# Two up projections of a gated MLP, accumulated side by side instead of one after the other

## The reference

```
xn2 = rmsnorm(x, ln2_w)
s   = x + (silu(xn2 @ W1) * (xn2 @ W3)) @ W2      # W1, W3: 512 x 1408, W2: 1408 x 512
out = x0 + s * silu(ffn(xn))                      # the gate comes from an earlier stage
```

## Time and profile before

| | us |
|---|---|
| median of 3 runs | 1926.0 (1924.37 to 1926.05) |
| the profiled execution, its time | 1922.71 |
| its span | 1921.0 |
| TensorE busy | 1780.7 (93%) |
| VectorE busy | 922.4 (48%) |
| ScalarE busy | 545.1 (28%) |
| mean granted TensorE clock | 0.978 |

### The profile page before, as it was taken

How to read it: one execution, slowest core, us unless ns; L and a number is a source line. 1 busy time by engine, 2 the same in 40 slices (tenths; PEclk the granted TensorE clock), 3 DMA queues, 4 the chain that set the end, 5 groups by cost and what they waited for, 6 DMA issues and landing times. The chain is left out here.

```text
span 1921.0 us, 24333 instructions
## 1 busy us (share of the span) xinstructions
PE 1780.7 (93%) x9104; PEld 1319.7 (69%) x9104; DVE 922.4 (48%) x1336; ACT 545.1 (28%) x887; POOL 403.5 (21%) x353
## 2 busy tenths in 40 slices
PE   4999999778999999999998749999999999999998
PEld 3878888654656666565656438787878787777776
DVE  4464454255777768576777455514141413132322
ACT  3223333232424335242523133212121212121211
POOL 5780000025425251533425000000000000000000
PEclk9999999989999999999999779999999999999999
DMA  6342321110011010101011032220202020202020
GB/s 144 99 109 76 98 66 66 44 55 28 1 71 66 5 71 0 71 0 71 22 44 44 1 121 93 77 109 0 109 0 109 0 109 0 109 0 109 0 88 22
DMA packets 49040, 110.89 MB, mean 58 GB/s; under 512 B 12704, under 2 KB 24048, under 8 KB 40816
## 3 DMA queue, kind: packets, MB, share of 16 engines
q1 hardware_dynamic: 45104, 89.44, 13.9%
q10 hardware_dynamic: 2304, 16.78, 2.1%
q0 software_dynamic: 1600, 4.25, 1.1%
HBM read 76.89 MB, written 33.57 MB: 58 GB/s over the span
## 5 line engine op out<-in xcount | busy, mean ns | idle before, releaser
L1228 DVE TENSOR_TENSOR m_h<-m_ps,m_silu 128x512 f32<-128x512 f32 x88 | 60.8, 691 | 431.1 <-PE m_ps L1381 431.1
L1379 PE MATMUL m_ps<-m_xshi,m_w1hi 128*128 128x512 f32 x352 | 142.8, 406 | 7.6 <-DVE m_xslo L1221 6.0
L1353 POOL TENSOR_TENSOR m_sq_sum<-m_sq 128x512 f32<-128x512 f32 x8 | 10.8, 1352 | 658.5 <-ACT m_sq L1290 658.5
L1307 ACT ACTIVATE m_silu<-m_ps 128x512 f32<-128x512 f32 x88 | 52.4, 596 | 336.8 <-PE m_ps L1381 335.9
L1379 PE MATMUL m_ps<-m_xshi,m_w3hi 128*128 128x512 f32 x352 | 139.1, 395 | 2.4 <-ACT m_silu L1307 2.4
L1380 PE MATMUL m_ps<-m_xslo,m_w1hi 128*128 128x512 f32 x352 | 139.5, 396 | 0.0
L1381 PE MATMUL m_ps<-m_xshi,m_w1lo 128*128 128x512 f32 x352 | 139.5, 396 | 0.0
L1381 PE MATMUL m_ps<-m_xshi,m_w3lo 128*128 128x512 f32 x352 | 139.0, 395 | 0.0
L1380 PE MATMUL m_ps<-m_xslo,m_w3hi 128*128 128x512 f32 x352 | 139.0, 395 | 0.0
L978 PE MATMUL a_att<-a_qx,a_lv 128*32 128x512 f32 (+1 forms) x512 | 104.1, 516 | 22.4 <-DVE a_qxd L689 20.3
L818 POOL TENSOR_TENSOR a_qx<-a_lv,hmask 128x512 f32<-128x512 f32 x64 | 87.4, 1365 | 154.2 <-PE a_att L978 98.2
(11 more groups left out here) (242 smaller groups left out, 4195.1 us busy)
## 6 DMA issues: line engine op xcount, KB each, us to landing
row<-scratch_xn SPq DMA_DIRECT2D x16, 1024.0 KB, 4.8
row<-scratch_xmid SPq DMA_DIRECT2D x16, 1024.0 KB, 7.0
m_xt<-in_L_attn_W SPq DMA_DIRECT2D x33, 256.0 KB, 3.4
f_xt<-in_L_attn_x SPq DMA_DIRECT2D x8, 1024.0 KB, 7.5
scratch_xn<-row SPq DMA_DIRECT2D x8, 1024.0 KB, 6.3
scratch_gate<-row ACTq DMA_DIRECT2D x8, 1024.0 KB, 3.9
scratch_xmid<-row ACTq DMA_DIRECT2D x8, 1024.0 KB, 3.9
row<-scratch_gate SPq DMA_DIRECT2D x8, 1024.0 KB, 9.8
```

What stands on the lines that cost most here:

```text
L1228: dve.tensor_tensor(h[n], dense.region(f"b{j}"), silu[n], ALU.mult).then_inc(dense.taken_sem(f"b{j}"), 1)
L1307: act.activation(silu[n], dense.region(f"a{j}"), ACT.Silu).then_inc(dense.taken_sem(f"a{j}"), 1)
L1379: pe.matmul(ps, wh, xh, start=k == 0, stop=False)
```

## The change

In `up`, the loops over the two projections and over the four slices change places. Before, the 12 matmuls of a are issued, then the 12 of b. After, each slice gives 3 matmuls of a and 3 of b, in their two PSUM regions in turn. The waits for the weights of both and for the free regions of both now stand ahead of the first matmul of the block; the wait for a slice of the input stands ahead of the slice's first matmul, as before. Each projection still signals with its last matmul, which for a is now the fourth from the end of the block.

```diff
--- before.py
+++ after.py
@@ -1367,19 +1367,22 @@
                 pe.matmul(ps, avg_all, sq_sum, start=True, stop=True).then_inc(mean.ready_sem("ms"), 1)
 
             def up(i, j):
-                for n, (ab, w) in enumerate((("a", w1), ("b", w3))):
+                pair = (("a", w1), ("b", w3))
+                for n, (ab, w) in enumerate(pair):
                     pe.wait_ge(s_wlo, 3 * j + n + 1)
                     pe.wait_ge(*dense.free(f"{ab}{j}", i))
-                    ps = dense.region(f"{ab}{j}")
-                    for k in range(KT):
-                        if j == 0 and n == 0:
-                            pe.wait_ge(*count.at("xslo", i, k + 1))
+                for k in range(KT):
+                    if j == 0:
+                        pe.wait_ge(*count.at("xslo", i, k + 1))
+                    xh, xl = (a[:, k, :] for a in xs_hl)
+                    for ab, w in pair:
+                        ps = dense.region(f"{ab}{j}")
                         wh, wl = (a[:, k, j * P:(j + 1) * P] for a in w)
-                        xh, xl = (a[:, k, :] for a in xs_hl)
                         pe.matmul(ps, wh, xh, start=k == 0, stop=False)
                         pe.matmul(ps, wh, xl, start=False, stop=False)
                         ins = pe.matmul(ps, wl, xh, start=False, stop=k == KT - 1)
-                    ins.then_inc(dense.ready_sem(f"{ab}{j}"), 1)
+                        if k == KT - 1:
+                            ins.then_inc(dense.ready_sem(f"{ab}{j}"), 1)
 
             def down(i, j):
                 pe.wait_ge(*count.at("hlo", i, j + 1))
```

## The result

The changed kernel takes 1944.8 us (median of 4 runs, 1942.5 to 1946.0), the kernel before 1926.0 (median of 4, 1924.4 to 1928.2): a ratio of 1.0095 with a 95% interval of 1.0078 to 1.0113, 18.8 us slower. The forecast was 1945. In the profile after, `up` is L1381 to L1383, `down` L1397 to L1399, the transposes L1423.

The account below looks back on a forecast made before the run. Inside a batch TensorE's own order was taken as the bound. Batch 0 3.8, its clock 1.2, seven seams 9.6 and clock falls 4.6 us sum to 19.2, taking 1926.0 to 1945 us, range 1936 to 1951.

Parts of the forecast that it names:

- Arithmetic: All blocks: the same 24 up matmuls in another order cost 0, bounds -2 to +2 us.
- Waits for a region inside a batch: Inside a batch: the down matmuls hide the later silu of a before the next block, cost 0.
- The head of block 1: Seam between batches: block 1 as a whole waits for silu 0, 0.31 us each, 7 times.
- The late chain of the seam: Seam: later silu 1 delays copy 0, low part, product 1 and the serial chain to down 0, 1.06 us each.
- Batch 0 without the clock: Batch 0: all 24 matmuls of block 1 wait for silu 0, then product 1 is held back; 3.8 us.
- the term that was small: Batch 0: granted clock low when block 1 starts after TensorE's idle time, about 1.2 us, bounds 0 and 3.
- The clock at the seams: Behind seams: granted clock falls at 3 of 7, 1.5 us each, 4.6 us in all.
- a fall at every seam: Rival at the seams: clock falls at all seven, 10.5 us instead of 4.6, time 1951; chance 0.1.
- The sum: Whole kernel: 3.8 + 1.2 + 9.6 + 4.6 = 19.2 us slower, forecast 1945 us.
- the seam that doesn't pay: Rival at the seams: copy 0 or the product not on the path, time 1933; chance 0.07.
- the disturbed loop: Rival in the steady loop: bank cycling makes the clock fall once each block, 132 us, 2058 in all; chance 0.02.
- No fall at the seams: Rival at the seams: the clock holds despite the idle time, time 1940.6 us; chance 0.2.

Follow-up runs that it names:

- the kernel with blocks 0 and 1: The new matmul order in blocks 0 and 1 of each batch alone, the old order in blocks 2 to 10: 1946.9 us, ratio 1.0109.
- the filled seam: The changed kernel plus matmuls without use in TensorE's two idle stretches at each seam between batches (three, then five): 1939.5 us, ratio 1.0067.

## Why the prediction was right, point by point

**Arithmetic, 0.** Right, and shown by the kernel with blocks 2 to 10 in the new order (0.9995) and by its steps of 0.233 us.

**Waits for a region inside a batch, 0.** Right: no wait for silu or product inside a batch, and the stretch from 1360 to 1380 is busy throughout at clock 1.00. In the Trainium skill, TensorE: Matmul & The Clock Gate, "A second HAM failure mode: psum-queue depth-cycling", cycling through banks goes with a clock that oscillates. With three matmuls to a bank no run here shows it inside a batch: from 10 us behind each of the first six seams to the next, the granted clock is 1.00 in the profiles of both kernels and of the one with blocks 2 to 10 changed. VectorE's product starts 0.22 to 0.28 us behind the block's end, where it was 0.19 to 0.27, and the 36 matmuls of a block take 8.40 us as before.

**The head of block 1, 0.31 us.** Slightly high: 0.15 for the start (0.38 instead of 0.23) and 0.11 for the next step (0.34 instead of 0.23), 0.26 together; silu 0 ended 0.05 us before the first matmul, not 0.12. The kernel with the later waits for b gives 0.22.

**The late chain of the seam, 1.06 us.** Right in each step, to 0.01 us, from silu 1 at U - 0.50 to down 0 at U + 4.66. Shown by the swap of copy 0 and silu 1, which takes back 1.03.

**Batch 0 without the clock, 3.8 us.** Its first matmul of block 1 came 0.72 us behind the start of silu 0, as in the earlier trace rows; from there 24 matmuls instead of 12, then the queue as at the seams, and down 0 1.04 us behind the end of product 1. Together with the clock it came to 5.8, where I had put 5.0. The wait for silu was 6.2 us and not about 7, since block 0 itself took 8.0 us instead of 7.2, with its clock low for longer; that cost nothing, as silu 0 starts 13.5 us behind the first up matmul (13.4 before). The clock is the term that was small: it was low from the wait on to 1150, so 4.1 us of block 1 ran at 0.43 us from the start of one matmul to the next. That is 4.1 x (1 - 0.233/0.43) = 1.9 us instead of 1.2, and leaves 3.9 for the rest. This term varies from one execution to another: with the same batch 0, down 0 comes 24.57 us behind the first up matmul in the profile of the kernel with blocks 0 and 1, and 25.79 in that of the filled seam, where the clock was low for 6.1 us of block 1, against 24.84 here.

**The clock at the seams, 4.6 us.** Three falls of 1.5 us were forecast (which is 4.5; unrounded 4.7); in the profile there were four of 1.1 to 1.4 (99.38 to 99.64 against 98.26), 5.1 together. A fall costs less than 1.5 where part of the low stretch lies on the fourth transposes and on idle time. The filled seam shows the sum: 5.3 us by the medians. How many seams it takes was an estimate, and it varies: 4, 4, 4 and 6 in the profiles of the four kernels whose seam is 4.66 us long with its gaps open, none in the profiles of the six others, where the gaps are filled or the seam is about 3.6 us or shorter. So a fall at every seam, which had 0.1, was nearly met in one profile. Which seams fall stays open. The comparison on which the term rested, few matmuls in a stretch, didn't decide it: the trace of before has 1.25 us of matmuls from 1140.70 to 1144.30, less than the 1.3 of the changed seam, at a clock of 1.00, and it stayed there until 1148.9.

**The sum.** 19.2 us; the stage grew by 20.5 in the profile, and the time by 18.8 in the medians. In the profile batch 0 is 0.8 over its term, the falls 0.5 over, the seven seams 0.4 under (9.2 us, 1.31 each), and 0.4 to 0.5 us arise behind the last batch's transposes, for which the sum had no term. The profiled execution came out at 1946.0, 4 us over the 1941.9 forecast for it: 2.7 of them are the stages ahead of the change, 1.3 these. It was the slowest of its four runs, while the profiled execution of before was 3.3 us under its median. The mechanism was right; that the median came within 0.2 us of 1945 is luck, since the number of falls was an estimate between 0 and 7, terms missed on both sides, and the runs themselves lie 3.5 us apart.

Of the rivals, the seam that doesn't pay and the disturbed loop are ruled out. "No fall at the seams" is what the filled seam shows as a kernel: 1939.5, where 1940.6 had been worked out.

## What to carry to other kernels

When two accumulations are run side by side, the first result comes later, here by 2.1 us, three quarters of the second's time; look not at the instruction that reads it but at what is queued behind that reader on its engine, at the place with the least cover. Before reordering matmuls, write down for each result the distance from ready to needed at every seam of the loop, not only in its steady part. And a serial chain that a wait shows seven times over is worth shortening for itself: taking one instruction out of it gained 1.38 us at each seam, where the order of the matmuls had nothing to give.

## What the runs showed of the hardware

Two idle pieces of 0.96 and 1.33 us in a 4.66 us seam brought the granted clock down at four to six of seven seams that were alike within 0.1 us; one piece of 1.33 us did so at none of 21 seams (before, blocks 2 to 10, copy 0 ahead of silu 1), and one of 2.36 us in batch 0 of the kernel before didn't either. Eight matmuls without use in those pieces kept it up, at no cost in time. After the 6.2 us wait in batch 0, the clock stayed low for 4.1 us of uninterrupted matmuls, and after 7.0 us in the kernel with the filled seam for 6.1.
